# A windowed-attention block on one core: the value tensor copied and transposed once instead of twice, and laid out by sixteen placing DMAs a strip

## The reference

```
x = x + conv(layernorm over channels of x)
    conv: for a roll of 0 and of 2, for each half of 32 channels:
      q, k, v = 1x1 products with qkv_w; 4x4 windows; 8 heads of 4 channels
      out = softmax(q k^T * scale + bias) v  +  3x3 depthwise filter of v
x = x + expert layer(layernorm of x)
    router softmax, the two best of 8 experts, weighted sum of their products
```

## Time and profile before

| | |
|---|---|
| Time, median of 3 runs | 3960.85 us (3948.16 to 3964.89) |
| The profiled execution: its own time | 3955.5 us |
| its span in the trace | 3953.7 us |
| PE busy | 3575.8 us, 90% |
| DVE busy | 3195.4 us, 81% |
| ACT busy | 2298.3 us, 58% |
| POOL busy, its issuing of DMAs counted | 1532.2 us, 39% |
| Mean granted clock of PE | 0.974 of full |

### The profile page before, as it was taken

How to read it: one execution, slowest core, us unless ns; L and a number is a source line. 1 busy time by engine, 2 the same in 40 slices (tenths; PEclk the granted TensorE clock), 3 DMA queues, 4 the chain that set the end, 5 groups by cost and what they waited for, 6 DMA issues and landing times.

```text
span 3953.7 us, 204756 instructions
## 1 busy us (share of the span) xinstructions
PE 3575.8 (90%) x83621; PEld 2122.4 (54%) x83621; DVE 3195.4 (81%) x7043; ACT 2298.3 (58%) x4708; POOL 1532.2 (39%) x2698
## 2 busy tenths in 40 slices
PE   3899999998999989999999999999899999999986
PEld 1655555555555555555555555555555555555542
DVE  3888888887888878888788878888888888888873
ACT  3766656565656555666566556666566666666640
POOL 2544444343434433434343434444344443444420
PEclk8999999999999999999999999999999999999986
DMA  2222222222222222222222222222222222222220
GB/s 38 74 79 74 72 75 71 76 71 72 74 73 73 76 69 69 80 73 74 64 77 71 75 68 76 70 77 71 74 69 77 70 77 70 78 71 77 70 57 22
DMA packets 216196, 279.22 MB, mean 71 GB/s; under 512 B 79872, under 2 KB 190512, under 8 KB 215216
## 3 DMA queue, kind: packets, MB, share of 16 engines
q1 hardware_dynamic: 141488, 152.22, 14.5%
q0 software_dynamic: 73728, 113.39, 10.3%
HBM read 95.46 MB, written 56.62 MB: 38 GB/s over the span
## 4 chain that ended last, share of the span: by engine, by line
PE 67%; DVE 13%; ACT 9%; issue 8%; SPq 1%; DVEq 1%; DMA 0%; ACTq 0%
PE bank L611 20%; PE bank L527 13%; PE bank L543 10%; DVE v2t L943 5%; PE bank L566 4%; PE bank L624 4%; PE bank L518 3%; PE bank L616 3%; PE bank L583 3%; DVE gx L899 3%; ACT row_inv L683 2%; PE bank L638 2%; ACT row_inv L681 2%; PE bank L643 2%; DVE yn L953 2%
## 5 line engine op out<-in xcount | busy, mean ns | idle before, releaser
L477 POOL DMA_DIRECT2D kx<-k_sb x1536 | 736.9, 487 | 1074.1 <-ACT k_sb L733 1062.0
L611 PEld LDWEIGHTS bank<-probT,vx 128*32 128x32 f32 x36864 | 831.2, 193 | 217.6 <-issue 204.6
L611 PE MATMUL bank<-probT,vx 128*32 128x16 f32 x36864 | 888.8, 235 | 6.3 <-issue 5.6
L527 PE MATMUL bank<-gx,expert_sb 128*128 128x384 f32 x1536 | 717.1, 549 | 196.0 <-DVE gx L899 196.0
L899 DVE TENSOR_TENSOR gx<-bank,yn 128x384 f32<-128x384 f32 x768 | 423.1, 551 | 538.4 <-PE bank L518 536.2
L543 PEld LDWEIGHTS bank<-kx,qx 32*32 32x32 f32 x36864 | 562.0, 107 | 323.5 <-issue 320.4
L543 PE MATMUL bank<-kx,qx 32*32 32x64 f32 x36864 | 663.1, 220 | 54.6 <-issue 45.0
L486 POOL DMA_DIRECT2D vx<-v2t x768 | 382.0, 504 | 637.3 <-PE bank L616 525.4
L495 POOL TENSOR_TENSOR lepe_p<-lepe_p,tap_sb 128x384 f32<-128x384 f32 x384 | 403.8, 1051 | 574.7 <-ACT tap_sb L748 570.7
L910 DVE SCALAR_TENSOR_TENSOR lepe<-vpad,lepe_sb,lepe 128x384 f32<-128x384 f32 x960 | 589.7, 614 | 0.0
L710 ACT ACTIVATE prob<-prob 128x512 f32<-128x512 f32 x576 | 363.7, 631 | 231.7 <-DVE prob L930 231.7
(11 more groups left out here) (100 smaller groups left out, 4641.9 us busy)
## 6 DMA issues: line engine op xcount, KB each, us to landing
vx<-v2t POOLq DMA_DIRECT2D x768, 96.0 KB, 2.8
kx<-k_sb POOLq DMA_DIRECT2D x1536, 24.0 KB
z<-fin SPq DMA_DIRECT2D x1344, 24.0 KB
xs<-in_x SPq DMA_DIRECT2D x96, 192.0 KB
xt<-in_x SPq DMA_DIRECT2D x192, 96.0 KB
z0t<-z SPq DMA_DIRECT2D x192, 96.0 KB
out_y<-y_out SPq DMA_DIRECT2D x192, 96.0 KB, 2.5
xs<-in_x SPq DMA_DIRECT2D x96, 139.5 KB
```

The source lines that it names most:

```text
L477: pool.dma_start(kx[to + m:to + C:4, r % 2, m, :], k_sb[at + m:at + C:4, r % 2, :])\
L527: MM(bank_f[:, 0:SPX], expert_sb[:, e, :], gx[:, e % 2, :], start=False, stop=(e == E - 1))\
L611: last = MM(bank_o[32 * c:32 * c + 32, at * TOK:(at + 1) * TOK], vx[:, kr % 2, :, at * 4 + c], probT[:, kr % 2, at, c * TOK:(c + 1) * TOK] ...
```

## The change

v is copied out of PSUM once, unmasked, into v_sb (384 columns, windows in order), and transposed once into vt. A partition of vt is then one of two neighbouring windows (`odd`) and one of 16 keys; its columns are head, pair of windows, channel in the head. Since partitions no longer hold a channel parity, the placing is done by DMAs: for each of 4 groups, for each target half x (parity of the head) and each source half odd (parity of the window) one DMA moves 16 partitions, four heads, 48 columns (192 bytes) each. That is 16 DMAs a strip in place of 4. vx gets a dimension `odd`, and L611 reads it there. The channel order in which the weights wv are set up changes to fit. The `LAG` of `spread_v` goes from 7 to 8 slots.

```diff
 LAG = dict(
-    spread_k=4, turn_v=5, place_bias=6, spread_v=7, score=7, shift=8,
+    spread_k=4, turn_v=5, place_bias=6, spread_v=8, score=7, shift=8,
...
-        "mask_v": (p[:, None] & 1) == np.arange(2)[None, :],
...
-        v2 = sb("v2", [128, 2, WIN, 2, TOK])
-        v2t = sb("v2t", [128, 2, 8, WIN, 4])
+        v_sb = sb("v_sb", [128, 2, SPX])
+        vt = sb("vt", [128, 2, 8, WIN // 2, 4])
...
-        vx = sb("vx", [128, 2, 32, WIN * 4])
+        vx = sb("vx", [128, 2, 32, 2, WIN // 2 * 4])
...
-        X_DMAS, Z_DMAS, TILE_DMAS, K_DMAS, V_DMAS = 5, 11, 7, 8, 4
+        X_DMAS, Z_DMAS, TILE_DMAS, K_DMAS, V_DMAS = 5, 11, 7, 8, 16
...
                 if st := s.strip("spread_v"):
...
                     for g in range(4):
-                        rows = slice(32 * g, 32 * g + 32)
-                        pool.dma_start(vx[rows, r % 2, g * 8:g * 8 + 8, :].rearrange("p q n -> p (q n)"),
-                                     v2t[rows, r % 2, :, :, :].rearrange("p q n k -> p (q n k)")).then_inc(v_spread[r % 2], 16)
+                        for x in range(2):
+                            for odd in range(2):
+                                to, at = g * CH + x * TOK, g * CH + odd * TOK
+                                pool.dma_start(vx[to:to + TOK, r % 2, g * 8 + x:g * 8 + 8:2, odd, :],
+                                               vt[at:at + TOK, r % 2, x::2, :, :].rearrange("p h n k -> p h (n k)"))\
+                                    .then_inc(v_spread[r % 2], 16)
...
-                                      vx[:, kr % 2, :, at * 4 + c],
+                                      vx[:, kr % 2, :, at % 2, at // 2 * 4 + c],
...
-                    for x in range(2):
-                        S.activation(v2[:, r % 2, :, x, :].rearrange("p n (r w) -> p n r w", w=SP),
-                                     windows(bank_p[0][:, 0:SPX]), ACT.Copy,
-                                     scale=const("mask_v")[:, x:x + 1]).then_inc(v2_made, 1)
+                    S.activation(by_window(v_sb[:, r % 2, :]), windows(bank_p[0][:, 0:SPX]), ACT.Copy).then_inc(v_copied, 1)
...
-                    V.transpose(v2t[:, r % 2, :, :, :].rearrange("p q n k -> p n k q"), v2[:, r % 2, :, :, :].rearrange("p n x i -> p (n x i)")).then_inc(v2t_made, 1)
+                    V.transpose(vt[:, r % 2, :, :, :].rearrange("p q n k -> p n q k"), v_sb[:, r % 2, :]).then_inc(vt_made, 1)
```

More of the change, by code:

```diff
@@ L266, in metaformer_block @@
         q_made, k_made, q_saved, k_saved = sem("q_made"), sem("k_made"), sem("q_saved"), sem("k_saved")
-        v2_made, v2t_made = sem("v2_made"), sem("v2t_made")
+        v_copied, vt_made = sem("v_copied"), sem("vt_made")
         k_spread, v_spread, spread_cleared = sems("k_spread"), sems("v_spread"), sem("spread_cleared")
@@ L464, in _ @@
             G.memset(kx[:, :, :, :].rearrange("p a c n -> p (a c n)"), 0.0).then_inc(spread_cleared, 1)
-            G.memset(vx[:, :, :, :].rearrange("p a c n -> p (a c n)"), 0.0).then_inc(spread_cleared, 1)
+            G.memset(vx[:, :, :, :, :].rearrange("p a c b n -> p (a c b n)"), 0.0).then_inc(spread_cleared, 1)
             pool.wait_ge(const_loaded, 16 * N_WEIGHT_DMAS)
@@ L480, in slot @@
                     k, r = st
-                    wait_alone(pool, v2t_made, k + 1)
+                    wait_alone(pool, vt_made, k + 1)
                     if s.later(r, 2):
@@ L579, in slot @@
                     pe.wait_ge(v_saved, k + 1)
-                    wait_alone(pe, v2_made, (k + 1) * 2)
+                    wait_alone(pe, v_copied, k + 1)
                     for g in range(4):
@@ L698, in slot @@
                     if s.later(r, 2):
-                        act.wait_ge(v2t_made, k - 1)
-                    for x in range(2):
-                        S.activation(v2[:, r % 2, :, x, :].rearrange("p n (r w) -> p n r w", w=SP),
-                                     windows(bank_p[0][:, 0:SPX]), ACT.Copy,
-                                     scale=const("mask_v")[:, x:x + 1]).then_inc(v2_made, 1)
+                        act.wait_ge(vt_made, k - 1)
+                    S.activation(by_window(v_sb[:, r % 2, :]), windows(bank_p[0][:, 0:SPX]), ACT.Copy).then_inc(v_copied, 1)
                     act.wait_ge(vo_made, k + 1)
@@ L788, in _ @@
                     some = heads_of(2, g).rearrange("p (h a b y) -> p b h a y", h=HD, a=2, b=2)[:, b]
-                    V.tensor_copy(wv[:, g * CH + 16 * b:g * CH + 16 * b + 16].rearrange("p (a h y) -> p h a y", a=2, y=2), some)
+                    V.tensor_copy(wv[:, g * CH:(g + 1) * CH].rearrange("p (h y b a) -> p b h a y", h=HD, y=2, b=2)[:, b], some)
                     last = V.tensor_copy(wo[:, 64 * b:64 * b + 64].rearrange("p (a g h y) -> p g h a y", a=2, g=4, y=2)[:, g], some)
@@ L939, in slot @@
                     k, r = st
-                    dve.wait_ge(v2_made, (k + 1) * 2)
+                    dve.wait_ge(v_copied, k + 1)
                     if s.later(r, 2):
                         dve.wait_ge(v_spread[r % 2], k // 2 * (V_DMAS * 16))
-                    V.transpose(v2t[:, r % 2, :, :, :].rearrange("p q n k -> p n k q"), v2[:, r % 2, :, :, :].rearrange("p n x i -> p (n x i)")).then_inc(v2t_made, 1)
+                    V.transpose(vt[:, r % 2, :, :, :].rearrange("p q n k -> p n q k"), v_sb[:, r % 2, :]).then_inc(vt_made, 1)
                 if yt := s.tile("tile_sum"):
```

## The result

The changed kernel takes 3900.54 us (median of 4 runs, 3893.59 to 3904.79) against 3962.87 us for the kernel before, measured beside it. The ratio is 0.9844, with a 95% interval of 0.9809 to 0.9879: 62 us faster. The forecast was 3835 us, that is 126 us faster. The direction and the range held, the size of the gain was half.

What follows compares the result with a forecast made beforehand. PE was taken to set the pace, with short waits for DVE. From 3955.5 us profiled, - 62 - 110 + 48 gives 3831.5; with 5.35 us for the median of runs, 3835 us, 8-in-10 range 3765 to 3935.

Steps and rivals of the forecast that it cites:

- The turn: DVE's transpose of v, halved to 384 columns, falls from 1.52 to 0.76 us, bounds 0.53 and 0.86.
- Both pauses at the expert matmul: PE's waits for gx at L527, one in each strip of a tile, both close: 62 and 110 us.
- The blocked gate step: DVE's L848 stands 0.45 us behind a POOL addition at a shared SBUF port; later additions free it.
- rival 3: Nothing to measure: both additions in DVE's dense stretch block it fully, 202 us; time near 3970 us, chance 0.09.
- The collisions of the late additions: POOL's additions, now behind sixteen DMAs, hit DVE's dense stretch and reach PE at L611: 0.5 us a tile, 48 us.
- The DMAs on POOL: Sixteen issues a strip at 0.53 us each, 8.5 us in place of 2.0; they fit in POOL's time.
- the slope between two rows: POOL's DMA issue costs 487 ns for 16 rows, 498 for 32, so the price is mostly per DMA.
- Rival 1: Dearer DMA issues make lepe_p late for DVE's filter step or POOL the bound: slower, 4085 us at 0.8 each, chance 0.14.
- The zero: Dropping one of ACT's two copies of v, 111 us of busy time, saves no time.
- Place A: Strip where PE pauses 0.65 us for gx after the turn: pause closes, 62 us; additions landing there cost nothing.
- rival 2: Half the gain: place B closes only in part, giving 0 to 40 us; 3860 to 3935 us, chance 0.20.
- place B: Other strip, where gate steps follow the turn and PE pauses 1.15 us for gx: pause closes, 110 us.

Runs made afterwards that it cites:

- e7: Kernel before, with each of POOL's additions cut from 384 to 16 columns: 3884.07 us, ratio 0.9805.
- e8: Kernel before, with POOL's two additions of a strip moved ahead of the four DMAs of v: 3882.48 us, ratio 0.9805.
- e2: Changed kernel, with each of POOL's additions cut from 384 to 16 columns, still behind the sixteen DMAs: 3749.5 us, ratio 0.9456.
- e1: Changed kernel, with POOL's two additions of a strip moved ahead of the sixteen DMAs of v: 3766.21 us, ratio 0.9517.
- e5: Changed kernel, with a second copy of v on ACT put back, into a spare tile: 3891.97 us, ratio 0.9809.
- e4: Kernel before, with each of its four DMAs of v split in four, same bytes: 4031.81 us, ratio 1.0178.

## Why the prediction was right in direction and half in size

Put side by side, in medians:

| | additions as they stood | cut to 16 columns | ahead of v's DMAs |
|---|---|---|---|
| before | 3962.6 | 3884.1 (e7) | 3882.5 (e8) |
| changed | 3900.5 | 3749.5 (e2) | 3766.2 (e1) |
| difference | 62 | 135 | 116 |

**The turn.** It took 568 ns (566 to 571), less than the 0.76 us that I took and near the lower bound of 0.53. Both pauses at the expert matmul closed, as forecast: 172 us of 196. Without collisions the new way of v is worth 116 to 135 us. The forecast's 129 (172 less the 43 of the blocked L848) lies between them.

**The blocked gate step.** Right as a mechanism and too small: 43 us forecast, 74 to 79 measured (e7, e8), and in e7 the filter steps and yn got shorter as well. The sentence of rival 3 that only one of a tile's four additions cost DVE time was wrong by that. Turn and gate step together, the change without collisions would have been worth 196 us (3962.6 to e1) to 213 us (to e2), where the forecast had 172.

**The collisions of the late additions.** This is the step that failed. The forecast saw that the additions would land in DVE's dense stretch and reach PE, and priced it at "0.5 us a tile, 48 us", by the nearest price, L848's 0.45. The runs show 134 us (e1) to 151 us (e2), 1.4 to 1.6 us a tile. So the gain was 24 to 41 us larger than forecast and the loss 86 to 103 us larger; the measured 62 is the difference of the two. Three things were missed. First, L848 had been hit by the tail of one addition; two additions back to back in a stretch that is full of operations with two SBUF inputs held it up for nearly their whole 2.1 us. The Trainium skill ("SBUF — State Buffer", who interferes with whom) says that a VectorE operation with two SBUF inputs and a GpSimd one that reads SBUF block each other for the whole instruction. The forecast had that bound and I put it at 0.09 as a case of its own; the trace agrees with it nearly, at 1.9 us of DVE time beside 2.08 us of additions in the tile shown. Second, the reader that mattered was not L611, but the gates' transposition L554, two groups earlier in the same stretch, which the forecast leaves out. Third, the clock: of the 21 longest pauses at L556 between 1000 and 3000 us, 18 were soon followed by half clock, and the three groups behind them grew by 51 us. The pauses at L527 that were closed had cost clock too, but less often (12 stretches against 20 in the same 2000 us); what that gave back was not measured by itself.

**The DMAs on POOL.** The issue took 515 ns mean (512 to 539) against 0.53 forecast, busy POOL 2715.7 us against 2770. The new pieces of 192 bytes cost no more than the slope between two rows said:

```profile
L487 POOL DMA_DIRECT2D vx<-vt x3072: 512/512/539, 72.6 to 3762.9; - x192
```

Rival 1 (late lepe_p, or POOL as the bound) is out: DVE waited 18.9 us for lepe_p, in 7 places. The sixteen DMAs cost little of their own (in e1 DVE waits 10.5 us for them); what they cost is that they stood ahead of the additions.

**ACT.** Its busy time fell by 73 us, not 111; the line of the copies alone went from 201.8 to 94.1 us. e5 shows the same gap: its second copy has 94 us on its line and raises ACT's total by only 52. Why the total moves less than the line stays open. The zero was right within what can be measured (e5).

**Place A.** "Nothing" was wrong as to DVE: fin L969 means 1269 ns after 549, as it falls on the additions (timeline of the changed kernel):

```profile
2061.00 2.09 DVE L969 TENSOR_TENSOR fin<-att,lepe 128x384 f32<-128x384 f32 x1
2061.65 2.29 POOL L497 TENSOR_TENSOR lepe_p<-lepe_p,tap_sb 128x384 f32<-128x384 f32 x2
```

What that costs PE was not measured by itself. It delays the stores of z behind it, and DVE's waits for the load z2t went from 6.4 to 24.3 us (3.3 in e1, 6.0 in e2); with the chain's shares of SP and z2t this speaks for a part of the loss, but no run took it apart.

**The case that came true.** By its time it is rival 2, half the gain, at 0.20, and that rival names collisions of 1 us a tile and more. Its mechanism is only half right, though: it had place B closing in part, and the pauses at L527 did close. What happened is nearer to rival 3 (chance 0.09), pauses closed at one line and new ones at another because both additions hold DVE for most of their length, only that its price of 202 us was 134 to 151 and the gain it was set against was larger. That the measured time lies in the forecast's range owes something to luck: two terms were too small, with opposite signs.

## What to carry to other kernels

When an engine's list gets longer ahead of an instruction, ask where that instruction will now land, and on the other engine read every line of that stretch and who waits for each, not only the line after it. In this kernel an addition of 1 us on GpSimd had to be priced at nearly its whole length where VectorE runs operations with two SBUF inputs back to back, and a pause of PE near 2 us with some 0.5 us of lost clock on top (51 us over 96 tiles). Here moving two additions ahead of a row of DMAs was worth 134 us, more than twice what the change itself had brought; the best version measured that computes the whole result is the change with that move, 3766 us, 4.8% faster than before.

## What was not expected of the hardware

- A VectorE operation with one small SBUF operand was held up too. A TENSOR_SCALAR of 128 x 6 took 153 to 165 ns in the kernel before. In e1 its line means 356 ns, and the row shows it ending with an addition:

```profile
2003.89 0.99 POOL L485 TENSOR_TENSOR lepe_p<-lepe_p,tap_sb 128x384 f32<-128x384 f32 x1 [5.22 <-ACT tap_sb L747]
...
2004.55 0.36 DVE L857 TENSOR_SCALAR gate_vec<-gate_vec 128x6 f32<-128x6 f32 x1
```

- In e4 the same operation took up to 1078 ns. In the rows below it ends 0.13 us before the additions begin, while POOL still issues v's DMAs up to 2028.45; what held it is not shown.

```profile
L860 DVE TENSOR_SCALAR gate_vec<-gate_vec x96: 153/171/1078, 205.4 to 4002.6; 128x6 f32<-128x6 f32 x96
...
2027.42 0.90 DVE L860 TENSOR_SCALAR gate_vec<-gate_vec 128x6 f32<-128x6 f32 x1
...
2028.45 2.35 POOL L497 TENSOR_TENSOR lepe_p<-lepe_p,tap_sb 128x384 f32<-128x384 f32 x2
```

- A DMA of 64 pieces of 192 bytes cost GpSimd 512 ns to issue, one of 32 rows of 3072 bytes 498 ns, one of 32 rows of 768 bytes 496 ns (e4), in medians.
- The transpose of 384 columns that writes runs of four took 568 ns, that of 768 which writes each element apart 1515 ns: 1.48 against 1.97 ns a column.
